# Relative-position band of attention: high and low part stacked in one 128-row product instead of two 64-row products per side

## Chip, cores and metric

One core of one Trainium2 chip. The metric is the device time of one execution in microseconds (us). Here "faster" and "slower" compare medians of runs of the two kernels on the same chip.

## What is computed

One transformer layer on eight sequences (B = 8) of 512 tokens with 256 features: x + attention(layernorm(x)), then a mixture of experts with 7 routed experts (two per token) and a shared one, on layernorm of the result. The attention has 16 heads of 16 features and a relative-position bias:

```python
scores = jnp.einsum('bhqd,bhkd->bhqk', q, k) * SCALING + position_bias
attn = jax.nn.softmax(scores, axis=-1)
ctx = jnp.einsum('bhqk,bhkd->bhqd', attn, v)
```

`position_bias[h, q, k]` depends only on k - q, and is constant for keys more than 90 positions away on each side. Everything is float32 in the reference.

## The kernel before, in words

The program has three parts that run one after the other: `project` (layer norm, the q, k and v projections, the table of biases by distance), `attend` and `finish` (output projection, routing, experts). The change lies in `attend` and in one helper that loads for it.

**Work of `attend`.** There are 32 items (NI), one for each group of four heads (HG = 4 groups) and each sequence. Four items with the same group make a quad, so two quads share a group. An item has 8 steps (STEPS): two pairs of heads times four tiles of 128 positions. A step makes, for the two heads ("sides") of one pair, scores and exponents of 128 x 512. Side 0 lives in SBUF rows 0 to 63 and side 1 in rows 64 to 127 of `q_st` and `k_st`.

For each step TensorE (the function under `@block.tensor` in `attend`) issues:

- `scores` (L793): one product per side, 48 rows, 512 columns, into `pS`. It is for a step 15 steps ahead. VectorE (L727) takes the minimum of bias minus scores over it, which is the negated maximum of the softmax. It waits for a free one of three `pS` banks through the semaphore `max_done`.
- `exponents`: one product per side of 62 rows and 512 columns (L810), which holds q, k, the maxima and the far bias. Then come the band products (L818), which add the bias of near distances. They multiply `place`, a 0/1 matrix that puts 64 rows at their half of the output, with `bandT`, the bias by distance, over only the columns that the band reaches. There is one product for each `half` of the tile, each `part` (high and low part of the bias, both fp32r) and each side: 2 x 2 x 2 = 8. `band(kh)` cuts them to 154, 218 or 244 columns. Over the four tiles the two halves have 154 and 218, 244 and 244, 244 and 244, 218 and 154 columns. They accumulate in `pE`, which has two pairs of banks, and ScalarE takes the exponential from there (L760).
- `values` (L832), in each second step, for the item before: four products of 128 rows by 32 output columns, one per head, each issued as two instructions because the operands are plain fp32.

The order on TensorE is written out in `slot` (L836 to L846). In an even step it is scores, exponents, band. In an odd step it is exponents, band, scores, values. Two steps together, which I call a double step, have 4 score products, 4 exponent products, 16 band products and 8 value instructions.

**Loads.** The SP queue issues them. `load_band` (L193 to L198) loads `bandT` for one head with one transfer of 64 rows, both parts, 244 elements each. There are 4 of them at the start of `attend` (L610), and one in each item of quads 0, 2 and 4 (L629), for the next group of heads. `exponents` waits for them through `band_ld` in the first item of a group (L801). `place` is built once in `project` (L374 to L378): `place[64 * side + i, half, 64 * half + i] = 1` for both sides. So its rows 0 to 63 and 64 to 127 already hold the same pattern.

Of the kernel before, what the change touches and what calls it, by code (L numbers as in the profile page):

```python
# [21 lines left out]
H, DH = 16, 16  # L22
TT = S // P
MC = D // P
HG, HPG = 4, 4
# [10 lines left out]
VLEN = 1024  # L36
TW = 896
HALF = P // 2
BW = 2 * (FAR - 1) + HALF
# [27 lines left out]
def band_start(kh):  # L67

    return S - 1 - (FAR - 1) - (HALF - 1) - HALF * kh
# [20 lines left out]
def raw(t):  # L90

    return t.bitcast(F32)
# [89 lines left out]
def attention_loads(g):  # L182

    near, bandT, q_st, k_st, v_raw = (g[n] for n in ("near", "bandT", "q_st", "k_st", "v_raw"))
    near_ld, band_ld, qk_ld, far_ld, v_ld = (g[n] for n in ("near_ld", "band_ld", "qk_ld", "far_ld", "v_ld"))
    q_dram, k_dram, v_dram = g["q_dram"], g["k_dram"], g["v_dram"]

    def load_near(sp, hg, j):

        rows = bass.AP(g["bias_dram"].tensor, (hg * HPG + j) * VLEN, [[1, P], [1, TW]])  # L190
        sp.dma_start(near[:, hg % 2, j], rows).then_inc(near_ld[j], 16)

    def load_band(sp, hg, j):  # L193

        pair, side = divmod(j, 2)
        lead = (hg * HPG + j) * VLEN + band_start(0)
        rows = bass.AP(g["bias_parts_dram"].tensor, lead, [[1, HALF], [H * VLEN, 2], [1, BW]])
        sp.dma_start(raw(bandT[HALF * side:HALF * side + HALF, hg % 2, pair]), rows).then_inc(band_ld[j], 16)  # L198

    PART = HG * HPG * DH * S  # L200

    def stacked(t, b, hg, side, part, inner):

        lead = (b * 2 + part) * PART + hg * (HPG * DH * S) + side * (2 * DH * S)
        return bass.AP(t.tensor, lead, [[2 * S, DH], *inner, [1, 2 * S]])

    def load_step(sp, quad, r, far):

        b, hg = 4 * (quad % 2) + r, quad // 2
        for side in range(2):  # L210
            row = HALF * side
            sp.dma_start(raw(q_st[row:row + 2 * DH, r]).rearrange("p j s -> p (j s)"),
                         stacked(q_dram, b, hg, side, 0, [[0, 2]])).then_inc(qk_ld[r], 16)
            sp.dma_start(raw(q_st[row + 2 * DH:row + KQ, r]).rearrange("p j s -> p (j s)"),
                         stacked(q_dram, b, hg, side, 1, [])).then_inc(qk_ld[r], 16)
            sp.dma_start(raw(k_st[row:row + 2 * DH, r]).rearrange("p j s -> p (j s)"),
                         stacked(k_dram, b, hg, side, 0, [[PART, 2]])).then_inc(qk_ld[r], 16)
            sp.dma_start(raw(k_st[row + 2 * DH:row + KQ, r]).rearrange("p j s -> p (j s)"),
                         stacked(k_dram, b, hg, side, 0, [])).then_inc(qk_ld[r], 16)
            if far:  # L220
                row = HALF * side + KQ + KM
                rows = bass.AP(g["far_dram"].tensor, ((quad // 2) * HPG + side) * (KF * S),
                               [[S, KF], [2 * KF * S, HPG // 2], [1, S]])
                sp.dma_start(raw(q_st[row:row + KF, r]), rows).then_inc(far_ld[r], 16)
        sp.dma_start(v_raw[:, r], v_dram[b, hg]).then_inc(v_ld[r], 16)

    return {"near": load_near, "band": load_band, "step": load_step}
# [338 lines left out]
def attend(nc, mk, g):  # L566


    place, max_dram = g["place"], g["max_dram"]
    ctx_dram, rden_dram, loads = g["ctx_dram"], g["rden_dram"], g["loads"]  # L570
    ctx_sb, den, c_out, rden_out = g["ctx_sb"], g["den_early"], g["c_out"], g["rden_out"][0]
    near, bandT, q_st, k_st, v_raw = (g[n] for n in ("near", "bandT", "q_st", "k_st", "v_raw"))
    near_ld, band_ld, qk_ld, far_ld, v_ld = (g[n] for n in ("near_ld", "band_ld", "qk_ld", "far_ld", "v_ld"))
    passed = g["passed"]
    with ExitStack() as ctx:
# [9 lines left out]
        pE = ps("pE", [P, 4, S], F32)  # L585
# [19 lines left out]
        with nc.Block() as block:  # L605
# [173 lines left out]
            @block.tensor  # L779
            def _(pe):  # L780
                pe.sem_inc(pv_done, PV0)
                pe.wait_ge(g["rows_set"], 32)

                def scores(m, r, rounds, step):

                    pair, t = divmod(step, TT)
                    if step == 0:
                        pe.wait_ge(qk_ld[r], 16 * 8 * rounds)
                    for side in range(2):
                        unit = 16 * m + 2 * step + side  # L790
                        rows = slice(HALF * side, HALF * side + KQ)
                        pe.wait_ge(max_done, MAX0 + unit + 1 - PS)
                        pe.matmul(pS[:, unit % PS], q_st[rows, r, pair, P * t:P * t + P], k_st[rows, r, pair],  # L793
                                  start=True, stop=True).then_inc(s_mm, 1)

                def exponents(n, r, step, quad, u, first):

                    pair, t = divmod(step, TT)
                    if u == 0 and t == 0 and quad % 2 == 0:
                        for side in range(2):  # L800
                            pe.wait_ge(band_ld[2 * pair + side], 16 * (quad // 2 + 1))  # L801
                    if step == 0:
                        pe.wait_ge(far_ld[r], 32 * (quad // 2 + 1))
                        pe.wait_ge(max_ld, 32 * (n + 1))
                    if not (first and step < 2):
                        pe.wait_ge(exp_done, STEPS * n + step - 1)
                    bank = 2 * (step % 2)
                    for side in range(2):
                        rows = slice(HALF * side, HALF * side + KS)
                        pe.matmul(pE[:, bank + side], k_st[rows, r, pair, P * t:P * t + P], q_st[rows, r, pair],  # L810
                                  start=True, stop=False, skip_group_check=True)
                    for half in range(2):
                        a, z = band(2 * t + half)
                        lead = a - band_start(2 * t + half)
                        for part in range(2):
                            for side in range(2):
                                rows = slice(HALF * side, HALF * side + HALF)
                                ins = pe.matmul(pE[:, bank + side, a:z], place[rows, half],  # L818
                                                bandT[rows, (quad // 2) % 2, pair, part, lead:lead + z - a],
                                                start=False, stop=half == 1 and part == 1, skip_group_check=True)  # L820
                    ins.then_inc(e_mm, 1)

                def values(n, par, t, first=False):

                    if t == 0:
                        pe.wait_ge(exp_done, STEPS * n + STEPS)
                        pe.wait_ge(v_ready, n + 1)
                        if not first:
                            pe.wait_ge(evac, n)
                    for j in range(HPG):  # L830
                        at = 8 * (j // 2) + 2 * t + j % 2
                        ins = pe.matmul(pC[32 * j:32 * j + 32], v_aug[:, par, t, j], prob[:, par, at],  # L832
                                        start=t == 0, stop=t == TT - 1, skip_group_check=True)
                    ins.then_inc(pv_done, 1)

                def slot(n, u, quad, first=False, last=False):  # L836
                    for step in range(STEPS):
                        ahead, other = divmod(STEPS + step + LEAD, STEPS)
                        early = step % 2 == 0
                        if early and not (last and u + ahead > 3):  # L840
                            scores(n + ahead, (u + ahead) % 4, quad + 1 + (u + ahead) // 4, other)
                        exponents(n, u, step, quad, u, first and u == 0)
                        if not early and not (last and u + ahead > 3):
                            scores(n + ahead, (u + ahead) % 4, quad + 1 + (u + ahead) // 4, other)
                        if step % 2 == 1 and not (first and u == 0):
                            values(n - 1, (u + 1) % 2, step // 2, first and u == 1)  # L846

                for step in range(STEPS + LEAD):
                    scores(step // STEPS, step // STEPS, 1, step % STEPS)
                for quad in range(QUADS):  # L850
                    for u in range(4):
                        slot(4 * quad + u, u, quad, first=quad == 0, last=quad == QUADS - 1)
                for t in range(TT):
                    values(NI - 1, 1, t)
# [812 lines left out]
```

## Time and profile before

| | us |
|---|---|
| runs of the kernel (3) | 856.91, 857.06, 858.42, median 857.06 |
| the profiled execution, own time | 865.07 |
| its span, first to last instruction | 863.3 |
| TensorE busy in the span | 775.4 |
| VectorE busy | 616.9 |
| ScalarE busy | 477.4 |
| attention: first to last band product | 123.9 to 520.6 |

The busy time of an engine is an average over stages with different limits. A product of TensorE is pipelined, and its end is modelled. So the busy times of products overlap, and the time that a product costs is read from the distance between starts. "Granted clock" is the share of TensorE's full 2.4 GHz, and 0.50 means 1.2 GHz.

### The profile page before, as it was taken

How to read it: one execution, taken by the hardware profiler on the slowest of the kernel's cores; microseconds unless marked ns; L12 is line 12 of the kernel's file. 1: busy time of each engine (PE TensorE's matmuls, PEld its weight loads, DVE VectorE, ACT ScalarE, POOL GpSimd, SP SyncE). 2: the span in 40 equal slices, each digit the busy share in tenths (PEclk: the TensorE clock that was granted, in tenths of full speed). 3: DMA queues.
4: the chain of work that ended last, by engine and by line, in shares of the span. 5: the costliest groups of instructions: out<-in, count | busy, mean ns of one | idle time of the engine just before them, and what ended most of it. 6: DMA issues, size and time to landing. Idle time of an engine off the chain costs nothing. (4 is left out here: it accounts for less than half of the span.)

```text
span 863.3 us, 18118 instructions
## 1 busy us (share of the span) xinstructions
PE 775.4 (90%) x6177; PEld 538.9 (62%) x6177; DVE 616.9 (71%) x1907; ACT 477.4 (55%) x720; POOL 258.7 (30%) x405
## 2 busy tenths in 40 slices
PE   5999889999999999999999996699999899999910
PEld 3777646666666666666656553456664489999910
DVE  5666586888888888888878831676663457777745
ACT  2444305666666666666666672455544167777700
POOL 1122011111111112111211110276565326666620
PEclk9999856999999999999999998899998799999965
DMA  4999882543555345443444814555322445555369
GB/s 120 293 342 354 284 212 75 141 111 102 143 149 137 99 114 156 137 118 112 124 144 126 281 55 120 153 190 175 125 99 74 135 133 158 163 156 167 117 247 379
DMA packets 74486, 140.73 MB, mean 163 GB/s; under 512 B 14504, under 2 KB 34624, under 8 KB 74222
## 3 DMA queue, kind: packets, MB, share of 16 engines
q1 hardware_dynamic: 62818, 116.90, 44.9%
q0 software_dynamic: 9792, 19.54, 6.9%
q10 hardware_dynamic: 1788, 3.18, 1.1%
q8 instruction: 49, 0.80, 0.4%
q14 instruction: 39, 0.32, 0.1%
HBM read 85.70 MB, written 56.78 MB: 165 GB/s over the span
## 5 line engine op out<-in xcount | busy, mean ns | idle before, releaser
L727 DVE CUSTOM_DVE_ANT_0 sums<-pS,near 128x512 bf16<-128x512 f32 x512 | 329.5, 687 | 54.5 <-PE pS L793 45.8
L760 ACT ACTIVATE prob<-pE 128x1024 f32<-128x1024 f32 x256 | 248.9, 1022 | 155.0 <-PE pE L818 154.8
L818 PEld LDWEIGHTS pE<-bandT,place 64*128 64x128 f32 x2048 | 169.9, 193 | 12.5
L818 PE MATMUL pE<-bandT,place 64*128 64x244 f32 (+2 forms) x2048 | 167.1, 275 | 0.0
L793 PE MATMUL pS<-k_st,q_st 48*128 48x512 f32 x512 | 140.9, 482 | 6.7 <-DMA k_st<-k_parts 4.1
L832 PE MATMUL pC<-prob,v_aug 128*32 128x512 f32 x1024 | 136.9, 609 | 1.0 <-ACT ctx_sb L768 1.0
L793 PEld LDWEIGHTS pS<-k_st,q_st 48*128 48x128 f32 x512 | 64.3, 196 | 117.3 <-DVE nmax L727 90.7
L810 PE MATMUL pE<-q_st,k_st 62*128 62x512 f32 x512 | 117.0, 410 | 1.9 <-issue 1.9
L1065 POOL DMA_INDIRECT expert_rows<-rb,xr x76 | 83.6, 1100 | 60.5 <-DVE rb L1243 48.6
L1049 POOL DMA_INDIRECT routed_rows<-xr,slot_i x64 | 65.5, 1024 | 44.5 <-DVE slot_i L1177 25.9
L810 PEld LDWEIGHTS pE<-q_st,k_st 62*128 62x128 f32 x512 | 58.6, 192 | 8.8 <-ACT prob L760 5.0
L1520 PE MATMUL pD<-w2p,hT 128*128 x456 | 63.5, 289 | 0.4 <-DVE hT L1236 0.4
L696 POOL DMA_DIRECT2D q_st<-negated_maxima x64 | 34.8, 548 | 94.7 <-DMA negated_maxima<-turned 94.7
L705 POOL COPY v_aug<-v_raw 128x256 f32<-128x256 f32 x32 | 12.7, 395 | 152.5 <-PE pC L832 152.3
L1520 PEld LDWEIGHTS pD<-w2p,hT 128*128 128x128 f32 x456 | 56.8, 191 | 0.6 <-issue 0.6
L491 PE MATMUL pQ<-xT,w_p 128*128 128x512 f32 x192 | 50.2, 413 | 2.9 <-DVE xT L402 1.5
L1236 DVE TENSOR_TENSOR hT<-ctx_sb,hT 128x512 fp32r<-128x512 f32 x38 | 26.3, 693 | 34.7 <-ACT hT L1366 34.7
L689 POOL DMA_DIRECT2D negated_maxima<-turned x32 | 22.5, 704 | 92.9 <-DVE turned L740 88.8
L491 PEld LDWEIGHTS pQ<-xT,w_p 128*128 128x128 f32 x192 | 36.5, 198 | 14.4 <-DVE qk L409 5.1
L727 DVE DVE_READ_ACCUMULATOR2_ANT nmax<- 128x1 f32 x512 | 42.4, 83 | 0.0
L1487 PE MATMUL pD<-w_sh,ctx_sb 128*128 128x256 f32 x128 | 41.7, 455 | 0.0
L832 PEld LDWEIGHTS pC<-prob,v_aug 128*32 128x32 f32 x1024 | 20.8, 108 | 32.8 <-issue 29.6
(169 smaller groups left out, 1018.4 us busy)
## 6 DMA issues: line engine op xcount, KB each, us to landing
xr<-routed_rows SPq DMA_DIRECT2D x38, 258.0 KB, 2.8
q_st<-q_parts SPq DMA_DIRECT2D x64, 128.0 KB, 2.7
k_st<-k_parts SPq DMA_DIRECT2D x64, 128.0 KB, 2.9
ctx<-ctx_sb SPq DMA_DIRECT2D x32, 256.0 KB, 2.8
q_parts<-qk SPq DMA_DIRECT2D x14, 512.0 KB, 8.0
k_parts<-qk SPq DMA_DIRECT2D x14, 512.0 KB, 7.7
near<-bias_by_distance SPq DMA_DIRECT2D x16, 448.0 KB, 5.6
xr<-expert_rows SPq DMA_DIRECT2D x12, 512.0 KB, 7.6
```

Of the source, the lines that this page charges most:

```text
L491: ins = pe.matmul(pQ[:, m % 2], w_p[:, a, w, c, P * h:P * h + P], xT[:, par, z, c], start=k == 0, stop=k == 5)
L696: pool.dma_start(raw(q_st[row:row + KM, m % RING]), max_dram[m].rearrange("a (p h) s -> h a p s", h=2)[side]).then_inc(max_ld, 16)
L727: dve.tensor_tensor_reduce(sums[:, r % 4], pS[:, unit % PS], near[:, hg % 2, j, lead:lead + S], -1.0, BIG, ALU.add, ALU.min, nmax[:, j, t: ...
L760: act.activation(prob[:, par, 2 * step:2 * step + 2], pE[:, 2 * (step % 2):2 * (step % 2) + 2], ACT.Exp).then_inc(exp_done, 1)
L793: pe.matmul(pS[:, unit % PS], q_st[rows, r, pair, P * t:P * t + P], k_st[rows, r, pair], start=True, stop=True).then_inc(s_mm, 1)
L810: pe.matmul(pE[:, bank + side], k_st[rows, r, pair, P * t:P * t + P], q_st[rows, r, pair], start=True, stop=False, skip_group_check=True)
L818: ins = pe.matmul(pE[:, bank + side, a:z], place[rows, half], bandT[rows, (quad // 2) % 2, pair, part, lead:lead + z - a], start=False, st ...
L832: ins = pe.matmul(pC[32 * j:32 * j + 32], v_aug[:, par, t, j], prob[:, par, at], start=t == 0, stop=t == TT - 1, skip_group_check=True)
L1049: pool.indirect_dma_start(xs_dram[:, :], bass.IndirectOffsetOnAxis(ap=slot_i[:, b, c, t:t + 1], axis=0), xr[:, b % XR, t, c], None).then_i ...
L1065: pool.indirect_dma_start(yc_dram[:, :], bass.IndirectOffsetOnAxis(ap=place_of, axis=0), y_rows(i)[:, t], None).then_inc(y_out[i % NXG], 16)
L1487: ins = pe.matmul(pD[:, t2, u], h_f[:, m, P * t:P * t + P], w_sh[:, 1, m], start=False, stop=m == 1)
L1520: ins = pe.matmul(pD[:, i % 2, t], hT[:, i % 2, a, TS * m + P * t:TS * m + P * t + P], w2p[:, bass.ds(expert, 1), z, m].rearrange("p a n - ...
```

## The change

High and low part of the band are put above each other in the 128 rows of the moving operand, so that one product of 128 rows adds both. The number of band products per step falls from 8 to 4. `bandT` keeps its size but has another layout: rows 0 to 63 are the high part and rows 64 to 127 the low part, for each side. `load_band` issues two transfers of 64 rows by 244 elements instead of one of 64 rows by 2 x 244, and the semaphore is waited for at twice the count. `place` is the same tile, now read in all its rows.

```diff
     def load_band(sp, hg, j):
         pair, side = divmod(j, 2)
-        lead = (hg * HPG + j) * VLEN + band_start(0)
-        rows = bass.AP(g["bias_parts_dram"].tensor, lead, [[1, HALF], [H * VLEN, 2], [1, BW]])
-        sp.dma_start(raw(bandT[HALF * side:HALF * side + HALF, hg % 2, pair]), rows).then_inc(band_ld[j], 16)
+        for part in range(2):
+            lead = (part * H + hg * HPG + j) * VLEN + band_start(0)
+            rows = bass.AP(g["bias_parts_dram"].tensor, lead, [[1, HALF], [1, BW]])
+            sp.dma_start(raw(bandT[HALF * part:HALF * part + HALF, hg % 2, pair, side]), rows).then_inc(band_ld[j], 16)
...
-                            pe.wait_ge(band_ld[2 * pair + side], 16 * (quad // 2 + 1))
+                            pe.wait_ge(band_ld[2 * pair + side], 32 * (quad // 2 + 1))
...
-                        for part in range(2):
-                            for side in range(2):
-                                rows = slice(HALF * side, HALF * side + HALF)
-                                ins = pe.matmul(pE[:, bank + side, a:z], place[rows, half],
-                                                bandT[rows, (quad // 2) % 2, pair, part, lead:lead + z - a],
-                                                start=False, stop=half == 1 and part == 1, skip_group_check=True)
+                        for side in range(2):
+                            ins = pe.matmul(pE[:, bank + side, a:z], place[:, half],
+                                            bandT[:, (quad // 2) % 2, pair, side, lead:lead + z - a],
+                                            start=False, stop=half == 1, skip_group_check=True)
```

## Rows read from the trace of the kernel before

**Rows 1.** First part of the page: busy us, share of the span, instructions

```profile
PE 775.4 (90%) x6177; PEld 538.9 (62%) x6177; DVE 616.9 (71%) x1907; ACT 477.4 (55%) x720; POOL 258.7 (30%) x405
```

**Rows 2.** Stretches of one double step each: busy us of PE, PEld, DVE, ACT, POOL; clock

```profile
204.99:208.18 3.19, 3.19 (x34) 2.11 (x32) 2.92 (x12) 1.92 (x3) 0.69 (x1) 1.00 0.65 155
208.18:211.20 3.02, 3.02 (x33) 1.81 (x32) 2.58 (x8) 1.95 (x3) 1.09 (x2) 1.00 0.54 152
```

**Rows 3.** Timeline of TensorE's products, one double step: start us, us, rows and columns

```profile
300.02 1.06 PE L832 MATMUL pC<-prob,v_aug 128*32 128x512 f32 x8
301.02 0.50 PE L793 MATMUL pS<-k_st,q_st 48*128 48x512 f32 x2
301.36 0.39 PE L810 MATMUL pE<-q_st,k_st 62*128 62x512 f32 x2
301.59 0.60 PE L818 MATMUL pE<-bandT,place 64*128 64x154 f32 x8
302.03 0.40 PE L810 MATMUL pE<-q_st,k_st 62*128 62x512 f32 x2
302.26 0.62 PE L818 MATMUL pE<-bandT,place 64*128 64x244 f32 x8
302.72 0.39 PE L793 MATMUL pS<-k_st,q_st 48*128 48x512 f32 x2
303.04 1.06 PE L832 MATMUL pC<-prob,v_aug 128*32 128x512 f32 x8
```

**Rows 4.** Timeline of the same band products, cut to 0.04 and 0.05 us

```profile
302.26 0.28 PE L818 MATMUL pE<-bandT,place 64*128 64x244 f32 x2
...
302.38 0.39 PE L818 MATMUL pE<-bandT,place 64*128 64x244 f32 x4
```

**Rows 5.** VectorE in the same double step: start us, us, idle before and releaser

```profile
300.13 0.69 DVE L727 CUSTOM_DVE_ANT_0 sums<-pS,near 128x512 bf16<-128x512 f32 x1 [0.30 <-PE pS L793]
...
300.75 0.69 DVE L727 CUSTOM_DVE_ANT_0 sums<-pS,near 128x512 bf16<-128x512 f32 x1
...
302.90 0.18 DVE L734 CAST nparts<-nmax 128x16 fp32r<-128x16 f32 x1
```

**Rows 6.** Timeline of products in finish: 24-row ones between 128-row ones

```profile
624.12 1.13 PE L1487 MATMUL pD<-w_sh,ctx_sb 128*128 128x256 f32 x4
625.18 0.38 PE L1485 MATMUL pD<-b2s,cTs 24*128 24x256 f32 x1
625.50 1.13 PE L1487 MATMUL pD<-w_sh,ctx_sb 128*128 128x256 f32 x4
...
624.66 0.38 PE L1487 MATMUL pD<-w_sh,ctx_sb 128*128 128x256 f32 x1
...
624.87 0.38 PE L1487 MATMUL pD<-w_sh,ctx_sb 128*128 128x256 f32 x1
```

**Rows 7.** Chain of waits: 12 products of 128 rows and 256 columns, fp32r

```profile
703.22 1.44 PE pU L1509 x12
```

**Rows 8.** SP queue's issues at the start of attend

```profile
110.86 2.60 SPq L198 DMA_DIRECT2D bandT<-bias_parts_by_distance  x4
113.50 0.60 SPq L212 DMA_DIRECT2D q_st<-q_parts  x1
```

**Rows 9.** Issues to landing of the band loads; what SP waits for, 160 to 450 us

```profile
bandT<-bias_parts_by_distance SPq DMA_DIRECT2D x16, 122.0 KB, 4.9
...
SPq L212 <- PE pE L818: 130.9, 24, 6.5
```

**Rows 10.** First item of attention: timeline of its products

```profile
123.31 0.80 PE L810 MATMUL pE<-q_st,k_st 62*128 62x512 f32 x2
...
127.43 0.79 PE L793 MATMUL pS<-k_st,q_st 48*128 48x512 f32 x1 [0.37 <-DVE nmax L727]
...
131.57 0.79 PE L793 MATMUL pS<-k_st,q_st 48*128 48x512 f32 x1 [0.36 <-DVE nmax L727]
```

**Rows 11.** Stretches: the first item, and the start of the program (columns as in rows 2)

```profile
124.00:144.00 20.00, 18.54 (x122) 15.32 (x122) 12.25 (x41) 9.90 (x10) 2.89 (x5) 0.50 0.35 90
...
0.00:40.00 40.00, 28.46 (x140) 20.92 (x141) 22.66 (x60) 14.41 (x23) 7.20 (x27) 1.00 0.67 191
```

## Prediction, made before the changed kernel was run

> **What bounds the kernel now.** I read the page first, then the attention stage alone, then one double step product by product. TensorE is busy for 90% of the span, VectorE for 71% [rows 1]. The average doesn't say who ends last in attention, so the stretches of one double step come next: TensorE has no idle time in them (3.02 of 3.02 us, 3.19 of 3.19 us), VectorE has 0.44 and 0.27 us of it, ScalarE over 1 us, and the granted clock is 1.00, the 2.4 GHz level [rows 2]. So in this stage a microsecond more on TensorE is a microsecond more of time, and one less is a gain until VectorE is full. VectorE starts back-to-back units 0.62 us apart, and before the first unit of this double step it waited 0.30 us for TensorE's scores [rows 5]. Four units and a small remainder are about 2.5 us of 3.02.
>
> Now one double step [rows 3]. Distances between starts are what things cost: values 1.00, scores 0.34, exponents 0.23, band 0.44, exponents 0.23, band 0.46, scores 0.32, sum 3.02. The band is 0.90 of 3.02 us, 30%.
>
> The decisive reading is how 8 band products fit into 0.46 us. In a stretch of 0.04 us two of them start, and the next group starts 0.12 us later, again with more than one product in it [rows 4]. The same holds of the exponents: two products of 512 columns take 0.23 us from start to the next kind [rows 3], and 512 columns at 2.4 GHz are 0.213 us. So the product of side 0 (rows 0 to 63) and that of side 1 (rows 64 to 127) stream together. The 8 products are 4 pairs, each about 0.112 us, where 244 columns alone stream in 0.102 us.
>
> **What the change does to the streaming: nothing.** Four products of 128 rows can't run in pairs, since each takes the whole height. They stream one after another: 4 x 244 columns, as the 4 pairs did. The nearest row for their pace is the expert product of 128 rows, 256 columns, also fp32r: 12 in 1.44 us, 0.120 each [rows 7], of which 0.107 is the stream. Band products of 244 columns should come at 0.11 to 0.12, narrower ones are held at about 0.11 by something that isn't the stream: the pairs of 154, 154, 218 and 218 columns would stream in 0.31 us and took 0.44 [rows 3]. I take 3 distances of 0.112 and a last stream of 0.098 us (235 columns on average), 0.434 per step; before, it was 0.45. Halving the count gains at most some hundredths of a us per step.
>
> **What it adds: two changes of the array's row layout per step.** Exponents and scores use 64-row halves, the band then the full 128 rows. Such a change has a price in the trace, in another place: in finish, one 24-row product stands between groups of four 128-row products. From group to group it is 625.50 - 624.12 = 1.38 us [rows 6]. Within a group the distance is 624.87 - 624.66 = 0.21 us, which for this plain fp32 product is twice 256 columns at 2.4 GHz, 0.213; the 24-row product streams 0.107. Unbroken that would be 4 x 0.213 + 0.107 = 0.96 us. So 0.42 us go into two changes, about 0.205 each. The rows show of what it is made: the last 128-row product starts at 624.87 and the 24-row one at 625.18, 0.31 instead of 0.213, so 0.10 is waiting for the array to empty; the 24-row one has 0.32 to the next instead of 0.107, another 0.10 of emptying and 0.11 of a weight load that nothing covers. Attention itself agrees. Values to scores to exponents is the one place where 128-row products meet 64-row ones now: the second pass of the values streams 0.427 and starts halfway, and scores take 0.34 to the next kind instead of 0.213 [rows 3], the same uncovered load. The Trainium skill, page "TensorEngine Tiling (Array Packing)", section Key Properties, says that changing the tiling mode, not just the tile, drains TensorE, and lists 64x128 and 128x128 as different modes. By that rule the sum is the one below; without it, it would be the first rival's. Rows 6 agree with it for 24 against 128 rows, and no row shows 64 against 128 with 128 output columns in both.
>
> **The sum.** A step from its exponents to what follows the band now: 302.03 - 301.36 = 0.67 and 302.72 - 302.03 = 0.69 us; over the four tiles about 0.675. After: 0.213 stream of the exponents, 0.205 for the change into the full layout, 0.434 band, 0.205 for the change back: 1.057. Difference 0.382 us. 248 steps (31 items of 8) x 0.382 = +94.7 us.
>
> The first item apart: its 8 steps run at clock 0.50, the 1.2 GHz level [rows 11], a double step takes 131.57 - 127.43 = 4.14 us, and TensorE waits 0.36 us in it for VectorE's maxima [rows 10], as the sides run apart from each other. Two changes per step, 0.2 to 0.3 us each at this clock, less the waits and the stagger that they absorb: I take +0.2 per step, +1.6 us, bounds 0 and +5.
>
> A gain: every fourth double step takes about 0.16 us longer (3.19 instead of 3.02 [rows 2]), in it VectorE does the turn of the maxima (L734 to L740, from 302.90 [rows 5]), and scores of side 1 come late. With a double step of 3.8 us VectorE has 1.2 us to spare, so this delay goes: 31 x 0.16 = -5.0 us. Bounds 0 and -5.
>
> Loads: SP issues 8 band transfers at the start instead of 4. Four took 2.60 us [rows 8]; eight halves cost between 2.60 and 5.2, so the loads of ring places 2 and 3 are issued up to 2.6 us later. They are wanted from 125 us on and were issued from 113.50 [rows 8]. The last band load lands about 4.9 us after issue [rows 9], by 121 us, and the first exponents stand at 123.31 [rows 10]. So zero, with +2.6 as the upper bound. The 12 later ones (24 after) are issued before a wait of up to 6.5 us for TensorE (130.9 us over 24 waits [rows 9]): zero. The waits on `band_ld` move to the doubled count and nothing else queues behind them than before. Bytes are the same.
>
> Covers: DVE and ACT only get more slack, and finish starts later, unchanged. Sum: 94.7 + 1.6 - 5.0 = +91.3 us. For the profiled execution that is 865.07 + 91 = 956; it was 0.9% above the median of the three runs. Against the median: 857.06 + 91.3 = 948.
>
> **Rivals.**
>
> *The two row layouts need no drain.* The place is the boundary exponents to band and back. The trace's prices are for 24 against 128 rows and for a change of rows and columns together, so 64 against 128 could be cheaper, down to nothing. Then what is left is 0.434 against 0.45, or, if the same `place` weights for both sides needn't be loaded twice, pure streaming: 0.31 in two tiles, 0.407 in the other two, a gain of 0.09 per step. Outcomes: 857 - 0.09 x 256 - 5 = 829 up to 865 (band products at 0.120). It ends faster than before when both boundaries together cost less than the band products gain, under 0.02 to 0.09 us per step, against 0.41 by rows 6. A halving of the band's 0.45 us with the count of products is excluded, as 976 columns need 0.407 us. Chance 0.04, three quarters of it on the faster side.
>
> *Half the price:* emptying is paid, but the load is pulled ahead and hidden: 2 x 0.10 x 248 = 50, less 5: about 902. Against it, the uncovered load after each change in rows 6. Chance 0.07.
>
> *Loads of full-height weights aren't hidden at all.* Then each band product costs 0.107 + 0.102 us: 4 x 0.209 instead of 0.434, +0.40 per step, 99 us more: 1047. The twelve 128-row products at 0.120 speak against it [rows 7]. The Trainium skill, page "TensorE: Matmul & The Clock Gate", section "What overlaps and what doesn't", says that a weight load overlaps a running product only where the row group differs, which would give this; rows 7 disagree. Chance 0.02.
>
> *The clock falls.* With 0.8 us of emptying and loading in a double step of 3.8, TensorE might not be granted 2.4 GHz, as in the first item [rows 11]. At 1.2 GHz throughout, a double step takes at least the 4.14 us of rows 10 plus values (2 us) and changes: above 6 us instead of 3.06, up to +380: 1000 to 1240. Against it: at the program's start TensorE is busy 28.46 of 40 us at clock 1.00 [rows 11]. Chance 0.03.
>
> **How the numbers follow.** The forecast has 0.84. Its own range: a change at 0.19 to 0.22 us gives -7 to +7, band products at 0.107 to 0.120 give -5 to +8, the first item, the turn and the start of the loads -2 to +9. Together about 930 to 968. Outside it lie the rivals' 0.16, and a little of the forecast's own chance, so this range is also the one that holds 8 in 10. A measurement of this kernel can tell about 0.2%, 1.7 us, from no change. Faster by more: 0.03; within: 0.01; slower: 0.96.
>
> **What would show it.** The timeline of a double step about 3.8 us long; exponents to band about 0.31 us instead of 0.23; four band products about 0.11 us apart, the first with an uncovered load ahead of it, so about 0.2 to the second; band to the next exponents about 0.2 instead of 0.11; weight loads that start with their product instead of ahead of it, at each boundary. VectorE's idle time per double step above 1 us, all on scores. The clock at 1.00 from the second item on. Wrong: a double step still near 3.0 us, or exponents to band still 0.23; a clock under 1.00 inside attention; finish changed in length.

## The result, and the profile after

The changed kernel takes 949.09 us (median of 4 runs, 946.45 to 960.74). The kernel before takes 856.98 us (4 runs) on the same chip. The ratio is 1.106 (95% interval 1.102 to 1.111), so the change is slower by 92 us. A ratio, here and below, is formed without runs in the chip's slower state (here that of 960.74 us), so it differs a little from the ratio of the medians. The profiled execution took 946.45 us, with a span of 944.6.

The first part of the page of the changed kernel answers to [rows 1]:

```profile
PE 864.0 (91%) x5153; PEld 535.9 (57%) x5153; DVE 621.6 (66%) x1907; ACT 492.2 (52%) x720; POOL 259.6 (27%) x405
```

TensorE has 1024 products fewer and is busy 89 us longer. VectorE and ScalarE do the same work as before, and their share of the span falls because the span is longer.

The timeline of TensorE's products of the changed kernel over one double step answers to [rows 3]. Its columns are start, duration, line and shape.

```profile
292.02 1.06 PE L831 MATMUL pC<-prob,v_aug 128*32 128x512 f32 x8
293.01 0.50 PE L794 MATMUL pS<-k_st,q_st 48*128 48x512 f32 x2
293.35 0.40 PE L811 MATMUL pE<-q_st,k_st 62*128 62x512 f32 x2
293.68 0.70 PE L817 MATMUL pE<-bandT,place 128*128 128x154 f32 x4
294.32 0.49 PE L811 MATMUL pE<-q_st,k_st 62*128 62x512 f32 x2
294.74 0.72 PE L817 MATMUL pE<-bandT,place 128*128 128x244 f32 x4
295.39 0.51 PE L794 MATMUL pS<-k_st,q_st 48*128 48x512 f32 x2
295.83 1.06 PE L831 MATMUL pC<-prob,v_aug 128*32 128x512 f32 x8
```

The double step is 295.83 - 292.02 = 3.81 us, where it was 3.02. Read the distances between starts in pairs, before against after. Values to scores is 1.00 and 0.99, and the scores that follow it take 0.34 in both. The first exponents took 0.23 to their band and now take 0.33. The band took 0.44 and 0.46 for eight products and now takes 0.64 and 0.65 for four. The exponents and scores that come after a band are longer as well: 0.42 instead of 0.23 (294.32 to 294.74) and 0.44 instead of 0.32 (295.39 to 295.83). Everything that touches an edge of the band is longer, and nothing else is.

The same timeline cut to short stretches shows products inside one band:

```profile
293.68 0.45 PE L817 MATMUL pE<-bandT,place 128*128 128x154 f32 x2
...
293.86 0.53 PE L817 MATMUL pE<-bandT,place 128*128 128x154 f32 x3
...
293.97 0.41 PE L817 MATMUL pE<-bandT,place 128*128 128x218 f32 x2
```

The second product starts 0.18 us after the first, the third 0.11 after the second. The first has its weight load uncovered, and the later ones cost what a pair of 64-row products cost. The view of the weight loads over the whole program counts the same edge (L817, the engine idle ahead of the load):

```profile
L817 PEld LDWEIGHTS pE<-bandT,place 128*128 128x128 f32 x1024 | 138.2, 195 | 79.8 <-issue 79.8
```

That is 79.8 us of idle time of the weight loads in front of 1024 of them. Put down to the 256 steps it is 0.31 us each. In the double step above, the load for the first band product starts at 293.68 us together with its product, and the load for the second starts while the first product runs. So the loads inside a band are issued ahead, and the one at the edge isn't. VectorE has the slack that was forecast. Its first unit after the values now waits 1.04 us for scores, where it waited 0.30 [rows 5]:

```profile
292.12 0.69 DVE L728 CUSTOM_DVE_ANT_0 sums<-pS,near 128x512 bf16<-128x512 f32 x1 [1.04 <-PE pS L794]
```

Where the 92 us lie can be read from starts in the two traces. From the first band product to the last start of the values is 402.0 us before (123.88 to 525.90) and 493.7 after (123.78 to 617.47), so +91.7. What follows took 337.4 and 327.1 us, though nothing in it was changed. About half of that difference is one stop before the first product of `finish`, 7.05 us before and 1.60 us after, and the mean granted clock of the part is 0.90 and 0.92. What sets the length of the stop is open. A second profiled execution of the changed kernel took 330.8 us for this part, and the traces of the other kernels lie between 329.8 and 337.0, so it moves without the change too. The two profiled executions differ by 81 us in span and the medians by 92, because the execution before lay 8 us above its median and the one after 2.6 us below.

### The profile page after: what moved, and what is told of

It reads as the page before. It is cut to its first block and busy times, and to the rows that moved or that the text cites. A ratio compares the mean times of both kernels' runs of the same rounds, so it can differ in the third digit from the quotient of the medians.

```text
span 944.6 us, 16086 instructions
## 1 busy us (share of the span) xinstructions
PE 864.0 (91%) x5153; PEld 535.9 (57%) x5153; DVE 621.6 (66%) x1907; ACT 492.2 (52%) x720; POOL 259.6 (27%) x405
## 5 line engine op out<-in xcount | busy, mean ns | idle before, releaser
L761 ACT ACTIVATE prob<-pE 128x1024 f32<-128x1024 f32 x256 | 262.6, 1026 | 219.9 <-PE pE L817 216.5
L817 PE MATMUL pE<-bandT,place 128*128 128x244 f32 (+2 forms) x1024 | 185.2, 304 | 0.0
L817 PEld LDWEIGHTS pE<-bandT,place 128*128 128x128 f32 x1024 | 138.2, 195 | 79.8 <-issue 79.8
L794 PEld LDWEIGHTS pS<-k_st,q_st 48*128 48x128 f32 x512 | 54.7, 193 | 129.9 <-DVE nmax L728 112.5
L811 PE MATMUL pE<-q_st,k_st 62*128 62x512 f32 x512 | 120.9, 460 | 0.0
L811 PEld LDWEIGHTS pE<-q_st,k_st 62*128 62x128 f32 x512 | 50.0, 190 | 21.3 <-issue 5.2
L1486 PE MATMUL pD<-w_sh,ctx_sb 128*128 128x256 f32 x128 | 36.2, 405 | 0.0
```

Of the source, the lines that this page charges most:

```text
L761: act.activation(prob[:, par, 2 * step:2 * step + 2], pE[:, 2 * (step % 2):2 * (step % 2) + 2], ACT.Exp).then_inc(exp_done, 1)
L817: ins = pe.matmul(pE[:, bank + side, a:z], place[:, half], bandT[:, (quad // 2) % 2, pair, side, lead:lead + z - a], start=False, stop=hal ...
L1486: ins = pe.matmul(pD[:, t2, u], h_f[:, m, P * t:P * t + P], w_sh[:, 1, m], start=False, stop=m == 1)
```

## The experiments

In each, "the kernel before" was run beside the variants on the same chip. Its median was 858.9, 858.7 and 858.9 us in the three groups.

### Fewer changes, same products

The changed kernel, with exponents of two steps ahead of the band products of both. This makes 4 changes of layout per double step instead of 6.

```diff
-    scores(step) ; exponents+band(step) ; exponents+band(step+1) ; scores(step+1) ; values
+    scores(step) ; exponents(step) ; exponents(step+1) ; band(step) ; band(step+1) ; scores(step+1) ; values
```

> The changed kernel with its band products grouped: exponents of two steps, then the 128-row band products of both, so a double step has 4 changes of the row layout instead of 6, with the same products. Theory (each change costs about 0.205 us, the products nothing more than before): double step 3.78 - 0.41 = 3.37 us, 123 of them, 949 - 50 = 899 us (893 to 905). Rival (the price sits in the full-height products themselves, 0.095 us each, for example in weight loads that nothing covers): nothing moves, 945 to 952. Rival (only emptying counts once the band is longer): 0.10 per change, 949 - 25 = 924.

Measured: 902.99 us, ratio 1.049 (1.043 to 1.055). The products are the same and the time is 46 us below the 949.09 of the changed kernel. The rivals at 945 to 952 and at 924 fall. The timeline shows the eight band products in one stretch:

```profile
302.50 0.50 PE L794 MATMUL pS<-k_st,q_st 48*128 48x512 f32 x2
302.83 0.64 PE L811 MATMUL pE<-q_st,k_st 62*128 62x512 f32 x4
303.40 1.12 PE L822 MATMUL pE<-bandT,place 128*128 128x244 f32 x8
304.45 0.49 PE L794 MATMUL pS<-k_st,q_st 48*128 48x512 f32 x2
```

Eight products take 304.45 - 303.40 = 1.05 us, with one uncovered load and one emptying. In the changed kernel each four take 0.64. The double step is 3.40 us, forecast 3.37.

The same order with 64-row products is the control.

> Control for the order: the kernel before, with its 64-row products, in the same grouped order. It has 2 changes of layout in a double step as before, so both theories expect 857 us (853 to 862); what it differs by is the price of the new order alone (ScalarE gets two steps at once, VectorE its scores at other distances).

Measured: 859.37 us, ratio 1.001 (0.998 to 1.005). The order alone costs nothing that can be told.

### Few full-height products, in the kernel before

The kernel before, with two 128-row products in the steps of the first pair of heads, for the first half of the tile. All the rest stays in 64 rows.

```diff
                     for half in range(2):
                         a, z = band(2 * t + half)
                         lead = a - band_start(2 * t + half)
+                        if half == 0 and pair == 0:
+                            for side in range(2):
+                                pe.matmul(pE[:, bank + side, a:z], place[:, half],
+                                          bandS[:, (quad // 2) % 2, side, lead:lead + z - a],
+                                          start=False, stop=False, skip_group_check=True)
+                            continue
```

`bandS` holds the stacked layout. The first build made room for it by cutting VectorE's throw-away sums from four buffers to one:

```diff
-        sums = sb("sums", [P, 4, S], BF16)
+        sums = sb("sums", [P, 1, S], BF16)
...
-                        dve.wait_ge(max_done, MAX0 + unit - 3)
+                        dve.wait_ge(max_done, MAX0 + unit)
```

> The kernel before, but in the steps of the first pair of heads only, and there only for the first half of the tile, the band comes from two 128-row products; the second half stays with four 64-row products. So 256 full-height products instead of the changed kernel's 1024, and two changes of layout in 128 of 256 steps. Theory (price per change): half of the 92 us, about 903 us (897 to 908). Rival (price per full-height product): a quarter, 880 us (875 to 885). It has one buffer for the throw-away sums of VectorE instead of four, to make room; the control beside it shows what that costs.

> Control for the run before it: the kernel before with one buffer for the throw-away sums, so each unit of VectorE waits for the one ahead of it. VectorE has 0.3 to 0.4 us of idle time in a double step of 3.02 us and the wait costs perhaps 0.05 to 0.1 us per unit: 857 to 870 us under every theory. Its excess is taken off the run before only where VectorE ends last there.

Measured: 922.88 us (ratio 1.074), and 907.20 us for the control (1.056, 1.050 to 1.061). My expectation for the control missed by 37 to 50 us. This is VectorE's timeline in the mixed kernel:

```profile
300.54 0.69 DVE L733 CUSTOM_DVE_ANT_0 sums<-pS,near 128x512 bf16<-128x512 f32 x1
...
301.39 0.69 DVE L733 CUSTOM_DVE_ANT_0 sums<-pS,near 128x512 bf16<-128x512 f32 x1
```

Units that wait for the one ahead start 0.85 us apart instead of 0.62 [rows 5]. Sixteen of them take 13.6 us, more than an item of the kernel before (about 12.3 us), so VectorE becomes the bound. So this pair decides nothing. I moved the sums into a tile that lies idle during attention, with four buffers as before, and ran it again:

```diff
-        sums = sb("sums", [P, 4, S], BF16)
+        sums = g["cn"][:, 1].rearrange("p c s -> p (c s)").bitcast(BF16).rearrange("p (a s) -> p a s", a=4)
```

> The mixed kernel again, without the VectorE wait that spoiled it: the throw-away sums keep four buffers, in room that lies idle during attention. Two 128-row products in each of 128 steps, all else in 64 rows: a quarter of the changed kernel's full-height products, half of its added changes of layout. Theory (per change): 46 us above the kernel before, 903 us (897 to 908). Rival (per full-height product): 23 us, 880 us (875 to 885).

Measured: 903.61 us, ratio 1.051 (1.045 to 1.058). The theory said 903 (897 to 908) and the rival 880 (875 to 885). Both kinds of double step stand next to each other in one trace:

```profile
302.38 1.06 PE L844 MATMUL pC<-prob,v_aug 128*32 128x512 f32 x8
303.38 0.50 PE L799 MATMUL pS<-k_st,q_st 48*128 48x512 f32 x2
303.72 0.40 PE L816 MATMUL pE<-q_st,k_st 62*128 62x512 f32 x2
303.95 0.62 PE L830 MATMUL pE<-bandT,place 64*128 64x244 f32 x8
...
305.43 1.06 PE L844 MATMUL pC<-prob,v_aug 128*32 128x512 f32 x8
306.42 0.50 PE L799 MATMUL pS<-k_st,q_st 48*128 48x512 f32 x2
306.76 0.40 PE L816 MATMUL pE<-q_st,k_st 62*128 62x512 f32 x2
307.09 0.45 PE L823 MATMUL pE<-bandS,place 128*128 128x154 f32 x2
307.47 0.48 PE L830 MATMUL pE<-bandT,place 64*128 64x218 f32 x4
307.79 0.40 PE L816 MATMUL pE<-q_st,k_st 62*128 62x512 f32 x2
...
309.21 1.06 PE L844 MATMUL pC<-prob,v_aug 128*32 128x512 f32 x8
```

The double step from 302.38 to 305.43 is 3.05 us, all in 64 rows. The one from 305.43 to 309.21 is 3.78 us, with two full-height products in each of its two steps. Two full-height products cost as much as the changed kernel's four. The price sits in crossing from one layout to the other and back.

### Half of the band's work, in either layout

The changed kernel with the second half of each tile's band left out (`for half in range(1)`):

> The changed kernel with only the first half of each tile's band: two 128-row products per step instead of four, two changes of layout as before. The second half's part of the bias is left out. Theory (products about 0.11 us each, the changes stay): 2 x 0.112 x 256 = 57 us less than the changed kernel, 892 us (885 to 898), still 35 us above the kernel before although it has half of the band's work. Rival (each full-height product costs 0.11 + 0.095): 2 x 0.205 x 256 = 105 us less, 844 us (836 to 852).

Measured: 900.00 us, ratio 1.047 (1.041 to 1.054). It is just above the theory's range of 885 to 898 and far from the rival's 844. The double step is 3.34 us, against 3.79 with all four products, so each product left out is worth 0.45 / 4 = 0.112 us. In the traces attention is 57 us shorter, as the theory said, and the part behind it 5 us longer (332.1 against 327.1). With half of the band's work it is still 41 us slower than the kernel before.

The kernel before with the low part left out (`for part in range(1)`), so half as many products and no change of layout:

> The kernel before with the high part of the band alone: four 64-row products per step in two pairs instead of eight in four; the low part of the bias is left out. So the count of products falls from 8 to 4 with no change of layout. Theory (a pair costs 0.112 us): 2 x 0.112 x 256 = 57 us less, 800 us, if TensorE stays the bound; VectorE needs about 2.5 to 2.6 us of a double step that would be 2.57, so it may take over: 800 to 815. Rival (halving the count doesn't help, as something else than the products sets the step): 845 to 857.

Measured: 832.71 us, ratio 0.966 (0.959 to 0.973). It is faster by 26 us, less than the 44 to 59 that I expected. The stretch from 300 to 350 us has its reason (busy us of PE, PEld, DVE, ACT, POOL, then the clock):

```profile
300.00:350.00 50.00, 50.00 (x428) 27.46 (x422) 47.20 (x156) 36.15 (x41) 10.16 (x19) 1.00 0.56 157
```

VectorE is busy 47.2 of 50 us. Most of its units start 0.61 us apart, and it waits 0.17 to 0.19 us for scores in a double step (at 304.47, 307.17 and 309.89 us). TensorE's loads for scores wait for VectorE in turn, 83 us in total between 160 and 420 us. Three double steps of 2.71 us are followed by one of 3.10 in which the maxima are turned. So even a halving of the band without any change of layout brought only 26 us here. That VectorE takes the rest is read from this trace, and no run tests it.

### Band next to values

```diff
-    scores ; exponents x2 ; band x2 ; scores ; values
+    scores ; exponents x2 ; scores ; band x2 ; values
```

> The changed kernel in this order per double step: scores, exponents of two steps, scores, band products of both steps, values. Band (128 rows, 128 output columns) and values (128 rows, 32 output columns) now meet. If a change of the output columns alone costs like one of rows, there are 3 changes in a double step against 4 of the grouped run: 3.40 - 0.20 = 3.20 us, about 878 us. If it is free, 2 changes as in the kernel before: about 3.0 us, 853 us. On top of both, the second scores of a double step come soon after the first and find only three banks: TensorE may wait up to 0.4 us for VectorE there, +50 us at most. So 853 to 928 in time; the verdict is read from the distance between the last band product and the first of the values (0.10 us: free; 0.2 us: emptying).

Measured: 942.84 us, ratio 1.097 (1.090 to 1.105), above the 853 to 928 that I gave. The timeline has both an edge and waits:

```profile
299.83 0.36 PE L822 MATMUL pE<-bandT,place 128*128 128x154 f32 x2
300.12 1.07 PE L836 MATMUL pC<-prob,v_aug 128*32 128x512 f32 x8
301.12 0.50 PE L794 MATMUL pS<-k_st,q_st 48*128 48x512 f32 x2
301.46 0.86 PE L811 MATMUL pE<-q_st,k_st 62*128 62x512 f32 x4
302.16 0.75 PE L794 MATMUL pS<-k_st,q_st 48*128 48x512 f32 x2
302.84 1.16 PE L822 MATMUL pE<-bandT,place 128*128 128x154 f32 x8
```

Two band products of 154 columns take 0.29 us to the values, where a distance of 0.11 and a stream of 0.064 would do. So 0.12 us is left for emptying, between two layouts that both have 128 rows and differ in their output columns. The second scores then take 302.84 - 302.16 = 0.68 us, where scores or exponents ahead of an edge took 0.33 in the changed kernel (293.35 to 293.68). The exponents take 0.70, where two pairs of 512 columns stream in 0.43. These 0.62 us are waits for banks: the loads for scores wait 129 us in total for VectorE between 160 and 580 us. The 3.20 us that I expected of three changes and these 0.62 give 3.82, and the double step takes 3.81 (300.12 to 303.93). VectorE in turn stands idle 1.25 us of it, because both pairs of scores come close together. The change saved was paid back as waits.

### A try at a version better than both

The kernel before, with values of two tiles together every fourth step and the scores spread over the steps between.

```diff
-                        if step % 2 == 1 and not (first and u == 0):
-                            values(n - 1, (u + 1) % 2, step // 2, first and u == 1)
+                        if step % 4 == 3 and not (first and u == 0):
+                            for t in (step // 2 - 1, step // 2):
+                                values(n - 1, (u + 1) % 2, t, first and u == 1)
```

> A try for a version better than both: the kernel before, all in 64-row products, with values of two tiles together every fourth step instead of one every second, and the scores spread evenly over the four steps between. That takes away two of four changes of layout in four steps, about 0.35 us in 6.1. Theory: up to 62 x 0.35 = 22 us less, 835 us, if VectorE is fed; but during 2 us of values no scores come, and three banks hold 1.9 us of work for it, so VectorE may end last: 835 to 857. Rival (the changes around the values cost nothing that can be saved): 857 or more.

Measured: 881.66 us, ratio 1.024 (1.018 to 1.031), slower, and above the 835 to 857 that I gave. The time alone fits the rival too, so this run doesn't show whether the changes around the values were saved. In its trace four steps take 6.31 and 6.82 us in turn, where they took 6.04 to 6.2. VectorE's timeline has this at the start of four steps:

```profile
300.50 0.69 DVE L727 CUSTOM_DVE_ANT_0 sums<-pS,near 128x512 bf16<-128x512 f32 x1 [1.18 <-PE pS L793]
```

It is starved for 1.18 us while 1.9 us of values run, and TensorE later waits for the free banks. Three banks of scores don't bridge the stretch. No version tried beats the kernel before. The only faster one leaves the low part out.

### The loads

The changed kernel with one transfer of 128 rows per head, beside the changed kernel once more. SP also waits for the first exponents of a group before it issues the next group's first load.

```diff
-        for part in range(2):
-            lead = (part * H + hg * HPG + j) * VLEN + band_start(0)
-            rows = bass.AP(g["bias_parts_dram"].tensor, lead, [[1, HALF], [1, BW]])
-            sp.dma_start(raw(bandT[HALF * part:HALF * part + HALF, hg % 2, pair, side]), rows).then_inc(band_ld[j], 16)
+        lead = (hg * HPG + j) * VLEN + band_start(0)
+        rows = bass.AP(g["bias_parts_dram"].tensor, lead, [[H * VLEN, 2], [1, HALF], [1, BW]])
+        sp.dma_start(raw(bandT[:, hg % 2, pair, side]), rows).then_inc(band_ld[j], 16)
```

> The changed kernel with one transfer of 128 rows per head instead of two of 64, so SP issues 4 band loads at the start as before, and one per item later. Theory (the loads lie beside VectorE's and TensorE's work): no difference from the changed kernel beside it, within 2 us. Rival (the 2.4 us of SP's queue at the start are on the path): 2 to 3 us faster.

> The changed kernel once more on this chip, as the partner of the run before it: 945 to 955 us.

Measured: 957.34 us (ratio 1.117, 1.107 to 1.127) against 951.94 (1.105, 1.096 to 1.115). It isn't faster, against the rival's 2 to 3 us, and the intervals overlap. The SP queue of the one-transfer kernel, then that of the changed kernel in the same group of runs:

```profile
110.63 6.26 SPq L198 DMA_DIRECT2D bandT<-bias_parts_by_distance  x4
```

```profile
112.29 4.99 SPq L199 DMA_DIRECT2D bandT<-bias_parts_by_distance  x8
```

Four issues held SP longer than eight in this execution. The timeline of the one-transfer kernel has two waits for loads, which the changed kernel's has not:

```profile
126.70 0.80 PE L812 MATMUL pE<-q_st,k_st 62*128 62x512 f32 x2 [3.42 <-DMA q_st<-negated_maxima]
...
133.16 1.22 PE L795 MATMUL pS<-k_st,q_st 48*128 48x512 f32 x3 [2.69 <-DMA k_st<-k_parts]
```

The first exponents start at 126.70 us against 123.97 in the changed kernel beside it, and the wait of 2.69 us lengthens the first item. Together that is 5.4 us, the whole difference of the medians. The late loads of `k_st` were issued by 124.4 us, ahead of the added wait, so the added wait isn't their cause. Why they and the maxima landed late is open. The run shows that this form of fewer transfers gains nothing. It doesn't show that the doubled count is free.

## Why the prediction was right, point by point

**The bound** was right. From the second item to the end of attention TensorE stands idle 2.9 us before and 0.8 us after, of 386 and 472 us, and attention is 91.7 us longer in the profiled executions.

**The streaming: nothing gained** was right. Later band products come 0.11 us apart in 128 rows, and the run with half of them gives 0.112 each, as taken in the sum. The pace of the 12 expert products of 0.120 [rows 7] was an upper bound that wasn't reached. The rival in which full-height loads aren't hidden, with 0.209 us per product, is refuted by the same distance. The Trainium skill, page "TensorE: Matmul & The Clock Gate", section "What overlaps and what doesn't", says that a weight load overlaps a running product only where the row group differs. The trace disagrees for this form: products of all 128 rows came 0.11 us apart with a load for each.

**The change of layout, 0.205 us** was right, and it decides the case. The forecast double step was 3.02 + 2 x 0.382 = 3.78 us, with four changes added, and the measured mean is 3.79. Taking two changes away gave 0.39 us per double step (3.79 to 3.40, forecast 0.41), so 0.195 each. The rival "half the price" falls with the grouped run, and "no drain" with it and the mixed one. The prediction called values to scores the one place where 128-row products met 64-row ones before. Scores to values is a second: 0.32 us in [rows 3], where 0.213 is the stream. It is there in both kernels and doesn't touch the sum. The rule of the Trainium skill, page "TensorEngine Tiling (Array Packing)", section Key Properties, holds here for 64 against 128 rows. For 128 against 32 output columns, both with 128 rows, 0.12 us of emptying was seen too.

**The turn of the maxima** was right. Double steps of the changed kernel are 3.77 to 3.81 us with none that stands out, where each fourth took 0.16 us more.

**The first item was mis-sized.** The sum had +1.6 us for its 8 steps, bounds 0 to +5. From its first exponents to those of the second item it took 16.72 us before (123.31 to 140.03) and 22.64 after (122.85 to 145.49), +5.9. The timeline of the changed kernel there answers to [rows 10]:

```profile
122.85 1.00 PE L811 MATMUL pE<-q_st,k_st 62*128 62x512 f32 x2
123.78 1.19 PE L817 MATMUL pE<-bandT,place 128*128 128x154 f32 x4
124.90 0.79 PE L811 MATMUL pE<-q_st,k_st 62*128 62x512 f32 x2
...
128.34 0.79 PE L794 MATMUL pS<-k_st,q_st 48*128 48x512 f32 x1 [0.36 <-DVE nmax L728]
...
134.01 0.79 PE L794 MATMUL pS<-k_st,q_st 48*128 48x512 f32 x1 [0.37 <-DVE nmax L728]
```

A double step there is 134.01 - 128.34 = 5.67 us against 4.14, which is 1.53 / 4 = 0.38 per change, about twice the price at full clock. The prediction took +0.2 us per step, and the runs show about 0.74. The waits of 0.36 us for VectorE are still there. I had expected them to absorb part of it.

**The other steps** made up for it. From the first exponents of the second item to the last values it is 472.0 us after (145.49 to 617.47) and 385.9 before (140.03 to 525.90), +86.1, where the sum had 94.7 - 5.0 = 89.7. Most of that gap is a wait that the sum doesn't have. TensorE stands still before the exponents of the 27th item, and then the clock is 0.50 for 3.4 us:

```profile
448.07 0.50 PE L793 MATMUL pS<-k_st,q_st 48*128 48x512 f32 x2
450.34 0.50 PE L810 MATMUL pE<-q_st,k_st 62*128 62x512 f32 x2 [1.76 <-issue]
...
454.58 0.61 PE L793 MATMUL pS<-k_st,q_st 48*128 48x512 f32 x2
```

That double step took 6.51 us instead of 3.02. The timeline names "issue" as the releaser, but the first exponents of an item wait for the load of its maxima (`max_ld`), and the last part of that load landed at 450.25 us, 0.09 us before the product started. Its two transfers were issued from 447.26 us:

```profile
447.26 1.09 POOL L696 DMA_DIRECT2D q_st<-negated_maxima  x2 [6.06 <-DMA negated_maxima<-turned]
```

It is no accident of one execution. The traces of the grouped 64-row order, of the kernel without the low part and of the values in pairs stop at the same place, for 1.88, 2.88 and 2.24 us. In the changed kernel the same load lands 2.2 us before it is used, so the longer double steps hide about 3.5 us of waiting. The last item makes about 1.3 us more of the gap: it has no scores, and its double steps grew by 0.58 us (2.54 to 3.12) instead of 0.76. Against this, the second item grew by 4.8 us (14.30 to 19.14) instead of 3.1, as the clock rose later in it.

So the price per step was right, and the sum came out at 948 against 949.09 with some luck: +4.3 us missed in the first item and 3.6 us too many in the rest nearly cancel. A changed length of `finish` had been named as a sign of being wrong, and it did change, by 10 us in the profiled executions. As said above, that part also moves without the change.

**The loads at zero** was right in the changed kernel. Eight issues took 5.00 us at the start (2.60 before), the first band product began at 123.78 us (123.88 before), and the only waits of TensorE in the first item are the four of 0.36 us for VectorE.

**The clock** was right in the main. The forecast had 1.00 from the second item on. It rose at 154.0 us, 8.5 us into the second item (before: at 144.2, 4.2 us into it), and then stayed at 1.00 to the end of attention (columns as in [rows 2]):

```profile
145.49:154.00 8.51, 8.51 (x30) 4.27 (x31) 4.62 (x16) 2.05 (x2) 1.79 (x3) 0.50 0.68 170
154.00:617.00 463.00, 462.19 (x2942) 228.51 (x2944) 320.89 (x1011) 270.83 (x277) 63.74 (x117) 1.00 0.38 109
```

The longer distances between products didn't cost it after that.

## What to carry to other kernels

Two products that use different halves of the array's rows already run together. Merging them into one full-height product saves no streaming, and the lower count of products alone was worth nothing here. Count the edges between layouts in the order of TensorE's work: at 2.4 GHz each edge between 64 and 128 rows cost about 0.2 us here (0.1 to empty and 0.1 for a weight load that nothing covers), as much as two products of 244 columns, so products of one layout belong together. An edge where only the output columns changed showed 0.12 us. Before moving products to save an edge, check what feeds the next engine: both reorderings that brought scores closer together or further apart gave back more than they saved. And look for waits that a slower stage will hide: they make its cost look smaller than it is.

## What I had not expected

Cutting a throw-away buffer from four to one cost 48 us. It made each VectorE unit wait for the one ahead: 0.85 us from start to start instead of 0.62. The slack that I read as 0.3 to 0.4 us per double step was smaller than four times that difference (0.92 us). And a change of layout costs nearly twice as much at clock 0.50 (0.38 us) as at full clock (0.195 to 0.205), so the same edge is dearest in stretches like the first item, which ran at 0.50 from end to end in both kernels.
